# A joint stage of second aggregation and dense experts over pairs of node tiles

## What is computed

```python
x = x + _L0_gnn_ref(_layernorm(x), src, dst, edge_weight, ...)   # two graph convolutions, 256 -> 128 -> 256
x = x + _L0_ffn_ref(_layernorm(x)[None], ...)[0]                 # 6 experts, three layers of 256, the best 2 are used
x = x + _L1_gnn_ref(_layernorm(x), edge_attr_256, ..., src, dst, ...)
x = x + _L1_ffn_ref(_layernorm(x)[None], ...)[0]                 # 8 experts, 256 -> 512 -> 256, the best 2 are used

# in _L0_gnn_ref, twice: agg = segment_sum(support[edge_src] * edge_weight, edge_dst)
# in _L0_ffn_ref: softmax over six logits, top 2, out = sum of w_k * expert_k(x)
# in _L1_gnn_ref: x = mish(nodes @ Wd + b); y = mish(edges @ We + b)
#                 agg = segment_sum(relu(x[src] + y), dst); mish((x + agg) @ Wo + b)
```

## Time and profile before

| | us |
|---|---|
| median of three runs | 4712.8 |
| lowest and highest run | 4711.4, 4717.1 |
| the profiled execution, span from first to last instruction | 4705.9 |
| TensorE busy | 3378.5 (72%) |
| GpSimd busy | 2947.3 (63%) |
| VectorE busy | 2342.6 (50%) |
| ScalarE busy | 1726.5 (37%) |
| mean granted TensorE clock | 0.751 of full speed |

### The profile page before, as it was taken

The page is one execution under the profiler, slowest core; times in us unless marked ns, Lnnn a source line. Parts: engine busy times, 40 slices in busy tenths (PEclk is TensorE's granted clock), DMA queues, the critical chain, the costliest instruction groups (busy, mean ns, idle before and its releaser), DMA issues. The chain is left out here.

```text
span 4705.9 us, 62078 instructions
## 1 busy us (share of the span) xinstructions
PE 3378.5 (72%) x15159; PEld 2951.3 (63%) x15159; DVE 2342.6 (50%) x6879; ACT 1726.5 (37%) x2410; POOL 2947.3 (63%) x2924
## 2 busy tenths in 40 slices
PE   5777767775677776776658866577767776667999
PEld 5666656664566665665446655566666666556887
DVE  5565555554566555555653335344443444582222
ACT  4444444443444444444323237222222222452333
POOL 2777777777677777777454430677777777363434
PEclk8777888787778888888769988555555555668999
DMA  4455554554455455544345541566666666234443
GB/s 139 153 162 160 157 162 156 158 155 131 150 162 162 153 160 159 160 151 144 110 123 89 107 100 58 177 205 204 204 206 204 205 205 201 92 129 119 97 91 63
DMA packets 317645, 696.83 MB, mean 148 GB/s; under 512 B 67233, under 2 KB 172091, under 8 KB 317420
## 3 DMA queue, kind: packets, MB, share of 16 engines
q1 hardware_dynamic: 170748, 402.05, 25.4%
q0 software_dynamic: 134560, 272.09, 23.9%
q10 hardware_dynamic: 12240, 21.66, 1.4%
HBM read 499.16 MB, written 198.82 MB: 148 GB/s over the span
## 5 line engine op out<-in xcount | busy, mean ns | idle before, releaser
L1151 POOL DMA_INDIRECT x_node<-node_table,src_sb x832 | 814.2, 979 | 411.8 <-issue 405.4
L562 PE MATMUL conv_pz<-conv_we,conv_edge 128*128 128x256 f32 x3360 | 1007.4, 467 | 44.6 <-PEq L76 44.6
L1165 PE MATMUL x_pa<-x_hot,x_node 128*128 128x64 f32 x3328 | 751.7, 423 | 328.4 <-PEq L76 327.7
L434 POOL DMA_INDIRECT conv_gath<-support_table,src_sb x832 | 787.8, 947 | 315.5 <-issue 302.9
L553 PE MATMUL conv_ps<-conv_hot,conv_gath 128*128 128x64 f32 x3328 | 550.3, 326 | 584.1 <-PEq L76 302.3
L434 POOL DMA_INDIRECT conv_gath<-hidden_table,src_sb x832 | 787.4, 946 | 263.8 <-issue 251.4
L1165 PEld LDWEIGHTS x_pa<-x_hot,x_node 128*128 128x128 f32 x3328 | 723.5, 331 | 356.8 <-issue 356.7
L553 PEld LDWEIGHTS conv_ps<-conv_hot,conv_gath 128*128 128x128 f32 x3328 | 516.0, 237 | 652.8 <-issue 340.8
L562 PEld LDWEIGHTS conv_pz<-conv_we,conv_edge 128*128 128x128 f32 x3360 | 796.2, 243 | 188.5 <-issue 45.9
L876 ACT ACTIVATE conv_q<-conv_q 128x1024 f32<-128x1024 f32 x210 | 221.9, 1057 | 1104.8 <-ACTq L76 1104.8
L1180 ACT ACTIVATE x_node<-x_node 128x1024 f32<-128x1024 f32 x208 | 219.7, 1056 | 856.1 <-ACTq L76 856.1
(11 more groups left out here) (197 smaller groups left out, 3873.8 us busy)
## 6 DMA issues: line engine op xcount, KB each, us to landing
conv_edge<-in_edge_t SPq DMA_DIRECT2D x210, 512.0 KB
edge_mish_table<-conv_neg SPq DMA_DIRECT2D x210, 512.0 KB, 3.0
x_neg<-edge_mish_table SPq DMA_DIRECT2D x208, 512.0 KB, 3.9
e_rows<-expert_rows SPq DMA_DIRECT2D x107, 272.0 KB, 3.3
conv_gath<-support_table,src_sb POOLq DMA_INDIRECT x832
conv_gath<-hidden_table,src_sb POOLq DMA_INDIRECT x832
x_node<-node_table,src_sb POOLq DMA_INDIRECT x832
expert_rows<-e_zeros ACTq DMA_DIRECT2D x12, 544.0 KB, 3.8
```

The costliest lines, as they stand in the source:

```text
L434: pool.indirect_dma_start(gath[g % SLOTS][:, j, :], None, table[:, :], bass.IndirectOffsetOnAxis(ap=c.src[:, col:col + 1], axis=0),).then_ ...
L562: last = pe.matmul(ps_z[r][:, j, :], edge[r][:, m, j * P:(j + 1) * P], we[:, m, :], start=m == 0, stop=m == KD - 1)
L1151: pool.indirect_dma_start(node[g % SLOTS][:, j, :], None, c.t3[:, :], bass.IndirectOffsetOnAxis(ap=c.src[:, col:col + 1], axis=0),).then_i ...
L1165: last = pe.matmul(ps_a[n][:, m, :], node[s][:, j, m * P:(m + 1) * P], hot[n][:, j, :], start=j == 0, stop=j == CG - 1)
```

## The change

The kernel keeps the first aggregation, and part 1 of dispatch and experts. Four stages (second aggregation, dispatch, experts and nodes) become one, `stage_mixing`. It runs over 27 parts of node tiles (`PARTS`: 1, 1, 22 pairs, 1, 1, 1), in steps u, and each step has six substeps j, one for each expert. All six experts are now applied to every row, weighted by shares that are zero for the four that were not chosen; lists, scatter and adding in DRAM go away. The groups that are due before a part can begin (`DUE`) are summed behind the first expert layer of the part two earlier, one or two in each substep. Its core, TensorE's substep (the lines left out in it are the small products: support, transposes, router, shared bias, logits, dense) and VectorE's `weighted`, which stands near the end of each of its substeps:

```diff
+PARTS = (1, 1) + (2,) * 22 + (1, 1, 1)
+DUE = tuple(min(GROUPS, -(-E * (t + n) // (N * CG)) + SLACK) for t, n in PARTS)
...
+            def step(k, u, j):
+                following, earlier = next_of(u, j), earlier_of(u, j)
+                if there(u):
+                    take(pe, hid_ready)
+                if there(following[0]):
+                    first_layer(*following)
+                for g in summed_in(u, j):
+                    segment(k, g)
...
+                if there(earlier[0]):
+                    take(pe, mid_ready)
+                if there(u):
+                    second_layer(u, j)
+                if there(earlier[0]):
+                    third_layer(*earlier)
...
+            def weighted(u, e):
+                take(dve, py_ready)
+                for s in range(PARTS[u][1]):
+                    here = xa[u % 3][:, s, :]
+                    last = nc.vector.scalar_tensor_tensor(here, py[:, s, :], shares[:, s, e:e + 1], here, ALU.mult, ALU.add)
+                link(dve, last, own)
+                dve.sem_inc(py_free, 1)
```

The first aggregation now takes only the even groups of edges; the odd ones have moved into the edge stage, here in the order of VectorE, ScalarE and TensorE:

```diff
+            def step(k, i, places, before):
+                message(k, i, 0)
+                if before:
+                    add(places[0], SLOTS - 1)
+                at = places[before:]
+                mish_end(0)
+                message(k, i, 1)
+                add(at[0], 0)
+                mish_begin(2)
+                message(k, i, 2)
+                add(at[1], 1)
+                mish_end(1)
+                message(k, i, 3)
+                add(at[2], 2)
+                mish_begin(0)
...
+                with act.Fori(0, IT - 1) as i:
+                    rectified(0)
+                    rectified(1)
+                    factor(2)
+                    rectified(2)
+                    rectified(3)
+                    factor(0)
+                    rectified(4)
+                    rectified(5)
+                    factor(1)
...
+                for r in range(MISH):
+                    segment(2 * r)
+                    segment(2 * r + 1)
+                    if r < products:
+                        product(r)
```

More of the change, by code:

```diff
@@ L3 @@
 from contextlib import ExitStack
+from itertools import count
 import numpy as np
@@ L1099, in stage_edges, with stage_mixing @@
[L1099 to L1102 removed]
+def stage_mixing(nc, c, table):
+    io, U = c.io, len(PARTS)
     with ExitStack() as ctx:
@@ new lines, in _ @@
+        @block.gpsimd
+        def _(pool):
+            with pool.Fori(0, load_passes(pool)) as k:
+                for g in range(GROUPS):
+                    if g >= SLOTS:
+                        pool.wait_ge(slot_free, g - SLOTS + 1)
+                    for j in range(CG):
+                        col = g * CG + j
+                        pool.indirect_dma_start(
+                            gath[g % SLOTS][:, j, :], None, table[:, :],
+                            bass.IndirectOffsetOnAxis(ap=c.src[:, col:col + 1], axis=0),
+                        ).then_inc(gathered[g % SLOTS], 16)
+                take(pool, slot_free, GROUPS)
@@ L1204, in add @@
                 dve.sem_inc(slot_free, 1)
-                dve.sem_inc(neg_free[s % RING], 1)
+                if s % 2 == 0:
+                    dve.sem_inc(neg_free[s // 2], 1)
                 here = c.feat[:, :, bass.ds(at, W)]
-                link(dve, nc.vector.tensor_tensor(here, here, ps_a[s % RING][:], ALU.add), add_own)
-            def step(k, i, slots):
-                places = places_of(nc, window, i * SLOTS - 1, slots, whole=True)
-                for s in range(slots):
-                    message(k, i, s)
-                    add(places[s], (s - 1) % SLOTS)
+                link(dve, nc.vector.tensor_tensor(here, here, ps_a[s % 2][:], ALU.add), own)
@@ new lines, in step @@
+            def step(k, i, places, before):
[13 more added lines that the diff above has]
+                mish_begin(0)
+                message(k, i, 4)
+                add(at[3], 3)
+                mish_end(2)
+                message(k, i, 5)
+                add(at[4], 4)
+                mish_begin(1)
@@ new lines, in last_step @@
+            def last_step(k, i):
+                places = places_of(nc, window, i * SLOTS - 1, TAIL + 1, whole=True)
+                message(k, i, 0)
+                add(places[0], SLOTS - 1)
+                mish_end(0)
+                message(k, i, 1)
+                add(places[1], 0)
+                message(k, i, 2)
+                add(places[2], 1)
+                mish_end(1)
+                message(k, i, 3)
+                add(places[3], 2)
+                add(places[4], 3)
+            for r in range(MISH):
+                dve.sem_inc(z_free[r], 1)
```

869 lines of the change are left out of this document (634 added, 235 removed).

## The result

| | before | after |
|---|---|---|
| median, us | 4714.0 | 4402.0 |
| lowest and highest of four runs | 4711.4, 4717.1 | 4399.5, 4413.3 |
| profiled execution, span | 4705.9 | 4401.9 |
| mean granted TensorE clock | 0.751 | 0.847 |

The account below looks back on a forecast made before the run. GpSimd's gather queue was taken to bound the aggregations and edge stage, TensorE the experts. 4705.9 - 454 (joint) - 10 (hidden) + 2 (first) + 196 (edge) = 4440, median 6.9 above: 4447 us, range 4320 to 4640.

Parts of the forecast that it names:

- Bound of the joint stage: Joint stage: TensorE sets it, over 90% busy at a clock over 0.95; gathers, 42.9 us for a pair, fit under.
- Hand-offs: Rival, joint stage: VectorE's some 60 waits each cost 0.25 us more, a pair takes 57 us, whole 4601 us; chance 0.25.
- the clock was not lost: Rival, joint stage: TensorE waits in every substep and its clock falls, making the kernel slower than before; chance 0.06.
- A pair: 50 us forecast: Joint stage, one pair of tiles: 45.5 us of TensorE work, 2.8 waits, about 1 stall, 0.7 waits for freed buffers.
- the wait of 0.19 us before some fifteen bursts: Joint stage, TensorE: a wait before a burst in some fifteen places of a pair, 2.8 us in all.
- the stall in substep 2: Joint stage: TensorE wants VectorE's and ScalarE's result after 11 us, 11.9 are needed; about 1 us for a pair.
- Lead-in: Joint stage start: parts 0 and 1 are too short to cover their gathers; 28 groups, 141 us, and 4 to start.
- VectorE's 41 us for a pair: Joint stage: VectorE's operations, waits and hand-offs sum to 41 us of 48, close to but not the bound.
- work hides them except the last small one: First stage: GpSimd's seven additions moved there are hidden, except the last and four small VectorE operations; +2 us.
- upper bound of 28: First stage: cost of the whole of the additions, if their place behind the spans in GpSimd's queue made them late.
- The edge stage: ScalarE's queue order, rectified(2) behind the factor, makes a cycle of 11.5 to 13.1 us for two groups; +196 us.
- 273 us "to the old time": In the lost-clock rival: distance from forecast to old time, 12.4 us for a pair, a mean joint-stage clock of 0.79.

Follow-up runs that it names:

- c1: New kernel with TensorE's two transposes of substep 2 moved behind its second and third layers, ScalarE's copies likewise; joint stage 1235.7 us, ratio 0.9262 to the kernel before.
- a1: New kernel without GpSimd's bias additions and their stores in the first stage; VectorE adds the bias in the joint stage; ratio 0.9365 to the kernel before.
- a4: As a1, but VectorE adds the bias to a part at the end of the step before; ratio 0.9331 to the kernel before.
- b1: New kernel with each edge-stage factor one rectified group later in ScalarE's queue; edge stage 1259.0 us, ratio 0.9317 to the kernel before.
- b2: New kernel with ScalarE's order as in b1 and TensorE's product between even and odd group; edge stage 1169.2 us, ratio 0.9129 to the kernel before.
- b5: New kernel with only TensorE's edge-stage product moved between even and odd group, ScalarE's order kept; edge stage 1324.5 us, span 4443.5 us, one run.
- a3: New kernel without GpSimd's bias additions in the first stage, stores kept; first gather at 89.3 us, span 4382.1 us, one run, profile only.
- d2: As d1, with parts of 1 and 24 pairs and each part due one group earlier; 4234.0 us, ratio 0.8997 to the kernel before.
- d1: New kernel with the changes of a4, b2 and c1 together; 4257.5 us, ratio 0.9050 to the kernel before.

## Why the forecast held, and where it was off

- **Bound of the joint stage.** Right, and by the mechanism given: TensorE, busy 1005 us of 1048 (96%) at a clock of 0.98, with GpSimd waiting for slots. Hand-offs did not bind (57 us for a pair), the clock was not lost.
- **A pair: 50 us forecast, 47.7 measured.** The mis-sized term is the wait of 0.19 us before some fifteen bursts, 2.8 us. It was read from the earlier trace rows, where a product waits for rows made just before; here the next work is ready and the bursts follow each other without a gap. Segments took 0.84 us, not 0.95 as in the earlier trace rows, another 1.0 for a pair. A transpose took 0.11 us, not 0.145. Against them: records at 0.216 us, not 0.2125 (+0.6), and the stall in substep 2 at 1.8 us, not 1. The last was named with its place, and c1 took it away; of the 37 us that this gained, some 15 are the clock. 164 x 0.216 + 8.5 x 0.84 + 14 x 0.11 + 0.4 = 44.5; with 1.8 that is 46.3. Most of the 1.4 us left to 47.7 is the clock: TensorE was busy 960.5 / 21 = 45.7 us for a pair, 1.2 more than 44.5, at a granted clock of 0.98, and 45.0 in c1 at 0.99, while these prices are from rows at the full clock. The forecast had no term for it.
- **The rest of the joint stage.** Lead-in 139 us (145 forecast), 22 pairs 1048 (1091.5), singles, drain and closing 86 (92). Sum 1273 against 1328.5. The bound of the lead-in was right: 28 groups of 5.05 us are 141.
- **VectorE's 41 us for a pair** were too many. Its busy time in the 22 pairs is 503 us, 23 for a pair. The two largest waits, before adds and `weighted`, come to 368 us in 990 (226.2 and 141.6 in its groups by line), 17.7 for a pair, so it needed at most 30. The many short gaps that were counted at 0.15 us each and the reading of places are inside that. It did no harm, since it was not the bound; a1 and a4 show that a pass of 0.7 us there still costs TensorE 0.3 to 0.5 us of waits for a pair.
- **First aggregation and hidden stage.** -13 for -10, in the hidden stage nearly all of it.
- **The first stage.** +17 for +2. The step that failed is "work hides them except the last small one": only GpSimd's own time was weighed, not what its additions do to VectorE's squares beside them, which lie on the chain of a unit: 16.5 us more, 7.6 of them in one square that waited for four additions. The reason given for the upper bound of 28, additions made late by their place behind the spans, was real, since it is why these stood ready one behind the other at 36.65; but it cost through VectorE and not through a late end, so the bound held in part by luck.
- **The edge stage.** +198 for +196, and for the reason given: 11.51 and 13.19 us for two groups, where 11.5 and 13.1 had been worked out from rows of before. The clock was 0.77, not 0.80, and the 12.2 us forecast for two groups in the mean stand against 12.1 measured. The forecast's list was incomplete in one point: behind ScalarE's order stood TensorE's, so the cause is a loop through both queues, and b1 alone could not show it; with b2 and b5 it shows.
- **A slip among the rivals.** The 273 us "to the old time" are taken from the span forecast 4440 to the median 4712.8; like with like they are 266, 12.1 for a pair, and the clock at which the gain would be gone stays 0.79. No chance changes by it.
- **The sum.** 4402 instead of 4447: -55 from the joint stage, +15 from the first, -3, +2 and +3 from aggregation with hidden stage, edge stage and the rest, together -38; the other 7 are the distance of the median from the profiled span, which was 0.1 us in the new kernel.

## To carry to other kernels

An edit that frees an engine can still be slowed by the order in its neighbours' queues: write the steady cycle out, operation by operation, from rows of the old kernel, and after moving one operation write it out again, since the wait can move to the next queue, as it did in b1. Before work is put on an idle engine "under cover", look at what its neighbours run at that moment and whether they share a way to memory, not only at its own time. A wait before a burst whose inputs are made just before it is no price for a burst whose inputs lie ready: 2.8 us for a pair had been forecast, and outside substep 2 there were 0.1.

## What had not been expected of the hardware

- A VectorE operation of 0.14 us (128x4, two inputs in SBUF) took 1.98 us while GpSimd added 128x1024 elements in 2.35 us, and 7.76 us beside four additions in a row, and ended with them to 0.02 us in the rows above. VectorE's statistics (four of 256 elements in 1.39 us, as ever) ran beside the additions unchanged. One operation with a single input was held too: the cast of 1x210 from SBUF to SBUF, 0.25 us in the kernel before and again in a3.

```profile
L305 DVE CAST base_row<-b_base 1x210 int32<-1x210 f32 x1 | 2.4, 2351 | 0.0
```

- The granted clock stood between 0.76 and 0.83 in the edge stages, with TensorE busy 79 to 87% of 1000 us, and at 0.98 in the joint stage with 96%. Small waits there cost by the clock as well: 23.4 us fewer waits in c1 came with 15.1 us less busy time for the same records.
- The same edge-stage code took 1165, 1169 and 1181 us in three profiles (d2, b2, d1), 16 us apart, where the clock reads 0.80 in all three. Of the 16 us 11 are busy time of the same 4992 records (958.5 and 969.9 us), which speaks for the clock; the rest is open.
